# A megakernel of linear attention and a gated feed-forward: the down projection in seven products for all eight pieces, and squares added on GpSimd ahead of the norms

## What is computed

```python
def fwht(x):                      # normalised Walsh-Hadamard transform over the last axis
    ...
xn = _layernorm(x)                                   # x: (8, 512, 512) f32
q, k, v = xn @ Wq.T + bq, xn @ Wk.T + bk, xn @ Wv.T + bv
kv_sum = cumsum((elu(k) + 1) * v, axis=1)
s = ((elu(q) + 1) * kv_sum * SCALE_A) @ Wo.T + bo
y = fwht(xn * SU_ug) / 64                            # 512 wide
up = y @ W_up.T * (Wscale_up * 64)                   # 2048 wide
gate = y @ W_gate.T * (Wscale_gate * 64)
z = fwht(silu(gate) * up * SU_dp) / 64               # 2048 wide
down = z @ W_down.T * (Wscale_dp * 64)               # 512 wide
out = x + s * silu(down)
```

## Time and profile before

| | |
|---|---|
| median of 3 runs | 1291.22 us (1289.54 to 1293.17) |
| the profiled execution's own time | 1291.18 us |
| its span | 1289.4 us |
| PE, PEld | 1259.5 us (98%), 570.7 us (44%) |
| DVE, ACT, POOL | 936.1 us (73%), 618.3 us (48%), 108.9 us (8%) |
| matmuls | 5896 |
| granted TensorE clock | 1.00 of full speed |
| moved by DMA | 226.21 MB, mean 175 GB/s |

### The profile page before, as it was taken

How to read it: one execution, slowest core, us unless ns; L and a number is a source line. 1 busy time by engine, 2 the same in 40 slices (tenths; PEclk the granted TensorE clock), 3 DMA queues, 4 the chain that set the end, 5 groups by cost and what they waited for, 6 DMA issues and landing times.

```text
span 1289.4 us, 16166 instructions
## 1 busy us (share of the span) xinstructions
PE 1259.5 (98%) x5896; PEld 570.7 (44%) x5896; DVE 936.1 (73%) x1417; ACT 618.3 (48%) x912; POOL 108.9 (8%) x159
## 2 busy tenths in 40 slices
PE   5999999999999999999999999999999999999998
PEld 3544444444444444444444444444444444444443
DVE  6989989878656777777883778776773767775724
ACT  5894655532245655552334555554233655454212
POOL 1000001131210000120022001000001000000001
PEclk9999999999999999999999999999999999999999
DMA  9534775777757356575378333323526433332423
GB/s 370 224 131 125 242 215 186 241 251 292 229 205 237 113 196 231 220 251 196 131 229 257 134 128 134 131 99 103 205 93 196 145 117 116 113 129 76 130 95 103
DMA packets 65472, 226.21 MB, mean 175 GB/s; under 512 B 7408, under 2 KB 17904, under 8 KB 50800
## 3 DMA queue, kind: packets, MB, share of 16 engines
q1 hardware_dynamic: 41840, 170.64, 36.7%
q0 software_dynamic: 16272, 42.48, 11.9%
q10 hardware_dynamic: 7280, 12.06, 2.7%
HBM read 171.64 MB, written 53.50 MB: 175 GB/s over the span
## 4 chain that ended last, share of the span: by engine, by line
PE 78%; DVE 9%; issue 5%; ACT 5%; DMA 3%; SPq 0%; DVEq 0%; ACTq 0%
PE bank L2450 40%; PE bank L2636 13%; PE bank L2330 12%; PE bank L2516 7%; PE bank L2541 2%; PE bank L2661 2%; ACT work L1229 1%; ACT work L1232 1%; DMA h_all<-scr_f 1%; DVE work L1675 1%; PE bank L2375 1%; PE bank L2561 1%; DVE work L1659 1%; DVE work L1665 1%; DVE work L1702 1%
## 5 line engine op out<-in xcount | busy, mean ns | idle before, releaser
L2450 PE MATMUL bank<-xops,ring 128*128 128x512 f16 x2772 | 603.2, 379 | 7.4 <-DVE work L1702 2.6
L2450 PEld LDWEIGHTS bank<-xops,ring 128*128 128x128 f16 x2772 | 269.4, 98 | 340.2 <-issue 11.1
L2330 PE MATMUL bank<-xops,ring 128*128 128x512 f16 x1008 | 225.2, 379 | 0.5 <-DVE ring L1831 0.5
L1212 ACT ACTIVATE work<-bank 128x512 f32<-128x512 f32 x198 | 117.8, 595 | 214.7 <-PE bank L2450 200.2
L1659 DVE TENSOR_TENSOR work<-bank,work 128x512 f32<-128x512 f32 x198 | 133.4, 686 | 113.0 <-PE bank L2450 99.8
L2636 PE MATMUL bank<-h_all,ring 128*128 128x512 f16 x768 | 166.8, 379 | 0.2 <-DVE work L1659 0.2
L2330 PEld LDWEIGHTS bank<-xops,ring 128*128 128x128 f16 x1008 | 98.1, 98 | 123.6 <-issue 9.1
L2636 PEld LDWEIGHTS bank<-h_all,ring 128*128 128x128 f16 x768 | 75.0, 98 | 91.0 <-DVE work L1659 0.7
L1259 ACT ACTIVATE h_all<-work 128x512 f16<-128x512 f32 x116 | 70.6, 624 | 62.6 <-DVE work L1702 62.5
L1711 DVE TENSOR_TENSOR h_all<-work,h_all 128x512 f16<-128x512 f32 x116 | 79.3, 686 | 5.7 <-ACT h_all L1259 4.4
L1665 DVE SCALAR_TENSOR_TENSOR work<-work 128x512 f32<-128x512 f32 x64 | 44.1, 690 | 51.2 <-ACT work L1232 50.8
(11 more groups left out here) (284 smaller groups left out, 1323.4 us busy)
## 6 DMA issues: line engine op xcount, KB each, us to landing
ring<-scr_g SPq DMA_DIRECT2D x72, 1024.0 KB, 4.8
ring<-scr_d SPq DMA_DIRECT2D x15, 1024.0 KB, 5.8
scr_g<-ring SPq DMA_DIRECT2D x22, 512.0 KB, 4.4
h_all<-in_ug_t SPq DMA_DIRECT2D x8, 1024.0 KB, 12.9
ring<-in_down_t SPq DMA_DIRECT2D x6, 1024.0 KB, 6.5
scr_g<-ring POOLq DMA_DIRECT2D x12, 512.0 KB, 5.7
work<-in_x_t SPq DMA_DIRECT2D x6, 1024.0 KB, 7.0
scr_g<-h_all POOLq DMA_DIRECT2D x12, 512.0 KB, 2.9
```

The source lines that it names most:

```text
L1212: act.activation(tile(g, j), chain_bank(g)[:, :], ACT.Copy).then_inc(copied, 1)
L2330: mm = pe.matmul(plain_bank(g, j)[:, :], at[:, s, 2 * dh + kk, r, :], xops[:, kk, xs, PLAIN_B[dh][c], :], start=(n == 0), stop=(n == len(t ...
L2450: mm = pe.matmul(to[:, :], weight_of(slot, s, b, kk), at, start=(a == 0 and m in (P1, P2, P5)), stop=(a == 5), skip_group_check=True)
```

## The change

1. `SEVEN` becomes 8: the down projection of pairs 2 and 3 is made in seven products for all eight pieces, 24 matmuls each. `rest` and its banks go. The order of the products is now P1, P2, P6, P7, P4, P5, P3, each for d = 0 and then 1. The units of weights' sums become eight, and the ring's loads of those pairs hold eight pieces each, with seven loads in place of eight.
2. The token sums of pieces 6 and 7 are laid down in `xops`, in blocks that the pair's last group has just finished with: ACT's copies of piece 6 wait for P2 of group 21, those of piece 7 for P7 of it. The next pair's operands (`x_high`), which go to the same `xops`, wait for P4 of the down projection. `x_high`, `t_high` and the gates on ACT, and the adds and operands on DVE, are written in a new order.
3. P1 waits for the low part of C11 of piece 7 (before: for all of piece 5), P2 for C21 of piece 7, P6 for the sums of piece 7 (before: of piece 5), P4 for ACT's copy of P7, P3 for DVE's add of P5 to C22.
4. GpSimd adds the four blocks of squares of each piece, first two and two, then the two sums (`sum_squares`), ahead of its all-reduce for the maximum. `norm(i)` waits for that and makes 4 matmuls of one column instead of 16. Two entries of `NORM_AT` move one tile later.

```diff
-GATE_ORDER = [(d, j) for j in (C11, C22, C21, C12) for d in range(2)]
+GATE_ORDER = [(d, j) for j in (C11, C21, C22, C12) for d in range(2)]
...
-SEVEN_FROM, SEVEN = 2, 6
...
+SEVEN_FROM, SEVEN = 2, FP
+DOWN_SLOTS = (P1, P2, P6, P7, P4, P5, P3)
+DOWN_ORDER = [(d, m) for m in DOWN_SLOTS for d in range(2)]
 DOWN_COPIES = ((0, P1), (1, P1), (0, P6), (1, P6), (0, P7), (1, P7))
-DOWN_SUMS = [(d, a) for a in ("22a", "11", "22", "12") for d in range(2)]
+DOWN_SUMS = [(d, a) for a in ("11", "22", "12") for d in range(2)]
...
-NORM_AT = (6, 7, 8, 8, 9, 10, 10, 11)
+NORM_AT = (6, 7, 8, 9, 10, 10, 11, 11)
...
+IN_RES = 6
...
+        def homes_late(i, s):
+            b = (T2, T3)[i - IN_RES]
+            return xops[:, :, s, b, :], xops[:, i - IN_RES, s, B21, :]
...
             def load_x(p):
                 sp.wait_ge(h_ready, 32 * p)
+                if p > SEVEN_FROM:
+                    sp.wait_ge(hidden_sums_ready, sums_of_hidden(p - 1, SEVEN - 1))
...
             def load_last_res():
+                sp.wait_ge(seven_done, down_to(PAIRS - 1, 1, P5))
...
+            def sum_squares(i):
+                at = squares(i).rearrange("p (m k n) -> p m k n", m=2, k=KB)
+                pool.wait_ge(squared, i + 1)
+                pool.tensor_tensor(at[:, :, 0:2, :], at[:, :, 0:2, :], at[:, :, 2:4, :], ALU.add).then_inc(squares_paired, 1)
+                pool.wait_ge(squares_paired, i + 1)
+                pool.tensor_tensor(at[:, :, 0, :], at[:, :, 0, :], at[:, :, 1, :], ALU.add).then_inc(squares_summed, 1)
...
             load_blocks(0)
+            for i in range(FP):
+                sum_squares(i)
             pool.wait_ge(max_ready, 1)
...
@@ ACT, x_high
+                        act.wait_ge(seven_done, down_to(p - 1, 1, P4))
...
@@ ACT, hidden_sums_high
-                elif i >= 4 and p < PAIRS - 1:
+                elif 4 <= i < IN_RES and p < PAIRS - 1:
                     act.wait_ge(stats_taken, 2 * p + 2)
...
+                act.wait_ge(product_done, products_to(p, GROUPS - 1, (P2, P7)[i - IN_RES]))
+                two, third = homes_late(i, HI)
+                act.activation(two, work[:, at:at + 2, :], ACT.Copy)
+                act.activation(third, work[:, at + 2, :], ACT.Copy).then_inc(hidden_sums_hi, 1)
...
@@ ACT, seven_and_o
-                if p < PAIRS - 1:
-                    x_high(p + 1, 0)
-                    t_high(p + 1, 0)
-                    x_high(p + 1, 1)
-                    t_high(p + 1, 1)
                 for d, j in GATE_ORDER:
+                    if p < PAIRS - 1:
+                        if (d, j) == (0, C21):
+                            x_high(p + 1, 0)
+                        elif (d, j) == (0, C22):
+                            t_high(p + 1, 0)
+                            x_high(p + 1, 1)
+                        elif (d, j) == (0, C12):
+                            t_high(p + 1, 1)
                     seven_gate(p, d, j)
...
@@ DVE, seven_and_o
+                for d in range(2):
+                    seven_add(p, d, "11")
                 if p < PAIRS - 1:
                     x_sums(p + 1, 0)
                     t_low(p + 1, 0)
-                for d in range(2):
-                    seven_add(p, d, "22a")
-                if p < PAIRS - 1:
-                    x_sums(p + 1, 1)
-                    t_low(p + 1, 1)
-                for d, a in DOWN_SUMS[2:]:
-                    seven_add(p, d, a)
+                seven_add(p, 0, "22")
+                if p < PAIRS - 1:
+                    x_adds(p + 1, 1)
+                seven_add(p, 1, "22")
+                if p < PAIRS - 1:
+                    x_low(p + 1, 1)
+                    t_low(p + 1, 1)
+                for d in range(2):
+                    seven_add(p, d, "12")
...
@@ DVE, last_sums
                 hidden_low(p, g, C21)
+                if p >= SEVEN_FROM:
+                    for part in range(2):
+                        hidden_sums(p, FP - 1, part)
+                    hidden_sums_low(p, FP - 1)
...
@@ PE, norm
-                pe.wait_ge(squared, i + 1)
+                pe.wait_ge(squares_summed, i + 1)
...
-                        for k in range(KB):
-                            mm = pe.matmul(bank[NORM_BANK][:, at:at + 1], at_squares[:, m, k, r, :], ones[:, :],
-                                           start=(k == 0), stop=(k == KB - 1))
+                        mm = pe.matmul(bank[NORM_BANK][:, at:at + 1], at_squares[:, m, 0, r, :], ones[:, :],
+                                       start=True, stop=True)
...
@@ PE, seven
                 if m == P1:
-                    pe.wait_ge(h_ready, 32 * p + 4 * SEVEN)
+                    pe.wait_ge(h_ready, 32 * p + 4 * SEVEN - 3)
                     wait_taken(pe, p, GROUPS - 2 + d, C21)
                 elif m == P2:
+                    pe.wait_ge(h_ready, 32 * p + 4 * SEVEN - 1)
                     pe.wait_ge(summed, 3 * nth(p, GROUPS - 2 + d) + 1)
                 elif m == P5:
                     pe.wait_ge(summed, 3 * nth(p, GROUPS - 2 + d) + 3)
+                elif m == P4:
+                    pe.wait_ge(seven_copied, down_copied_to(p, d, P7))
+                elif m == P3:
+                    pe.wait_ge(seven_summed, down_summed_to(p, d, "22"))
```

More of the change, by code:

```diff
@@ L220, in slot_of @@
         return RING[n % len(RING)]
-    return LATER_RING[(LOADS * (p - SEVEN_FROM) + n) % len(LATER_RING)]
+    return LATER_RING[(loads_of(p) * (p - SEVEN_FROM) + n) % len(LATER_RING)]
 def dmas_of(p, n):
-    return 2 if p >= SEVEN_FROM and GROUPS <= n < GROUPS + 2 * KB else 1
-ALL_LOADS = [(p, n) for p in range(1, PAIRS) for n in range(LOADS)]
+    return 2 if p >= SEVEN_FROM and GROUPS <= n < GROUPS + len(DOWN_SLOTS) else 1
+ALL_LOADS = [(p, n) for p in range(1, PAIRS) for n in range(loads_of(p))]
 def loads_into(p, n):
@@ L733, in load_seven @@
                         sp.wait_ge(unit_stored[u], 16 * UNITS)
-                if m == R11:
-                    to = ring[:, slot, :].rearrange("p (c e n) -> p c e n", c=2, e=KB)
-                    for half in range(2):
-                        sp.dma_start(to[:, half, :, :], scr_d[2 * half + 1, :, :, 1024 - 256 * REST:1024]) \
-                            .then_inc(slot_loaded[slot], 16)
-                    return
                 to = ring[:, slot, 0:512 * SEVEN].rearrange("p (d n) -> p d n", d=2)
@@ L866, in _ @@
             for p in range(1, PAIRS):
-                for n in range(LOADS):
+                for n in range(loads_of(p)):
                     load(p, n)
@@ L1729, in hidden_sums_low @@
                 dve.tensor_tensor(at[:, LO, :], tile(g, C12), at[:, HI, :], ALU.subtract).then_inc(h_ready, 1)
-                three = work[:, 4 * (g % 3):4 * (g % 3) + 3, :]
+                a = 4 * (g % 3)
                 dve.wait_ge(hidden_sums_hi, sums_of_hidden(p, i))
-                dve.tensor_tensor(home(i)[:, :, LO, :], three, home(i)[:, :, HI, :], ALU.subtract) \
-                    .then_inc(hidden_sums_ready, 1)
+                if i < IN_RES:
+                    dve.tensor_tensor(home(i)[:, :, LO, :], work[:, a:a + 3, :], home(i)[:, :, HI, :], ALU.subtract) \
+                        .then_inc(hidden_sums_ready, 1)
+                    return
+                (two_high, third_high), (two, third) = homes_late(i, HI), homes_late(i, LO)
+                dve.tensor_tensor(two, work[:, a:a + 2, :], two_high, ALU.subtract)
+                dve.tensor_tensor(third, work[:, a + 2, :], third_high, ALU.subtract).then_inc(hidden_sums_ready, 1)
             def use(p, g, j):
@@ L2480, in group @@
                     for d, m in DOWN_ORDER[1:]:
-                        if m < R11:
-                            seven(p, d, m)
-                        else:
-                            rest(p, d, m)
+                        seven(p, d, m)
                 elif g + 1 == GROUPS:
```

80 lines of the change are left out of this document (32 added, 48 removed).

## The result

| | before | changed |
|---|---|---|
| median | 1291.16 us (4 runs, 1289.54 to 1293.17) | 1327.71 us (4 runs, 1326.81 to 1328.88) |
| ratio | | 1.0283, 95% interval 1.0265 to 1.0301 |
| profiled execution: time, span | 1291.18, 1289.4 us | 1327.84, 1326.0 us |
| matmuls | 5896 | 5776 |
| granted TensorE clock, mean | 1.00 | 0.985 |

The account below looks back on a forecast made before the run. PE's list of matmuls was taken to bound the kernel (busy 1259.5 of 1289.4 us). Terms 16.3 - 5.2 - 0.3 + 8.2 + 4.4 = +23.4 on 1291.2 gave 1314.6 us, range 1297 to 1332.

Parts of the forecast that it names:

- Start and switches: Norms on GpSimd: a switch of instruction kind costs 9.35 us, before the first add (start 40.35) and before the all-reduce.
- Duration of a block: Norms: GpSimd's two adds per block take 3.6 us, between 2.0 and 5.3; PE leaves the last norm 14.4 us late.
- my first rival: Norms: GpSimd adds and two-input SBUF DVE instructions exclude each other, 14 us taken, 1329 us in all; chance 0.23.
- Which path ends the stretch: First pair: last norm, all-reduce, DVE's scales (+16.7 us), then ACT's K reads make PE 16.3 us late.
- P1's wait: Sevens: P1 waits for the eighth piece's low tile behind DVE's queue, +4.1 us in each of two pairs, +8.2.
- P3's wait: Sevens, third pair alone: P3 waits for DVE's late add of C22, +4.4 us.
- The clock: Rival: after each PE wait above 4 us the clock falls, four times, 10.4 us in all, 1325 us; chance 0.12.
- Matmuls and units: Sevens: 24 fewer matmuls, -5.2 us, one wait gone, -0.3; two more units of weights' sums costed at nothing.
- Cover holds: Rival: helpers have room at each new wait, so PE pays only its matmuls, 1283 us, faster; chance 0.07.

Follow-up runs that it names:

- the runs with one add: Kernel before plus only GpSimd's first add of squares per block, norms of 8 matmuls: 1305.39 us; with four DVE adds moved later too: 1302.19 us.
- the repaired kernel: Changed kernel with norms of before, piece 6 sums later, C22 adds earlier, last group's C11 tile ahead of the add awaiting P5: 1287.21 us, ratio 0.9965.
- the two kernels with such waits: Changed kernel with only the norms as before: 1301.09 us; the same with DVE's adds of C22 moved ahead: 1297.19 us.
- the filled: Changed kernel with norms as before, plus 15 unused matmuls ahead of P1 in both pairs and P3 in the third: 1296.73 us, ratio 1.0046.

## Why the prediction came out as it did

Direction and range were right (1297 to 1332, 0.88 for slower), the time was 13 us short. By its own steps:

- **Start and switches.** I took 9.35 for each. The first measured 8.11 (39.13 in place of 40.35), the second 5.86. Both were too high, by 1.2 and 3.5 us; the first of these hid a little of the next error.
- **Duration of a block: the step that failed.** I took 3.6 for the middle of 2.0 and 5.3. Alone it would have been a good figure: 3.3. But five of the eight took 5.1, one 4.6, the first and the last 4.1, in turns with DVE. PE left the last norm 22.8 us late, not 14.4. Of GpSimd's 38.5 us from first add to last, 8 x 3.3 = 26.4 are the adds' own; 12 are exclusion. This was my first rival, at 0.23. Its 1329 us lie only 1.3 from the measured time, but by luck: it priced exclusion alone, and of the 13 us missing from the forecast 9.2 are the clock. I had weighed it down because the trace of before, as I read it, showed GpSimd's powers beside adds that read a bank or beside nothing. One of the three does lie beside a DVE instruction with two inputs in SBUF:

```profile
798.46 1.69 POOL L895 TENSOR_TENSOR rstd<-var_eps,minus_half 128x8 f32<-128x8 f32 x1 [16.68 <-DVE var_eps L1550]
```

```profile
799.48 0.68 DVE L1729 TENSOR_TENSOR h_all<-work,h_all 128x512 f16<-128x512 f32 x1
```

Neither of them is longer for it. The evidence was thus a little better than I wrote, and still not enough: a power of 8 elements says nothing of adds of 1024. Why it does not keep DVE waiting as those do, no run here shows.
- **Which path ends the stretch.** I followed PE's last norm, the all-reduce, DVE's scales and ACT. Here the last norm itself decided, 22.8 against 21.3 for the scales; my term had it the other way about. With shorter adds the scales, through DVE's own queue, decide (the runs with one add), a path that I had not priced at all: I had stretched GpSimd only.
- **P1's wait:** 4.1 twice forecast (the terms listed there add up to 3.9), 3.63 twice measured. The size was right, the reason half right. I named the seventh piece's sums; they are 0.75 of it, and the other 2.9 is DVE waiting in order for P5. The queue that I listed had "one add" in it, and I gave it a duration but not its releaser.
- **P3's wait:** 4.4 forecast (its listed terms add up to 4.6), 3.84 measured, and the cause confirmed by moving DVE's adds.
- **The clock:** costed at nothing in the sum, a rival at 0.12 with 10.4 us. Measured 1.7 behind the norms and 3.0, 2.9 and 1.6 in the sevens, 9.2 in all. Rival and forecast were both true, so their terms should have been added: a forecast with four such waits in it owed the clock something. That 9.2 is close to the rival's 10.4 is partly luck: its price was taken from transposes in a stretch whose granted clock reads 1.00, and its condition, waits above 4 us, was not met by any of the four (3.20 to 3.84). The Trainium skill's "TensorE: Matmul & The Clock Gate" (Part 1) said that idle PE falls to half its clock; by that rule, the trace agrees, with a granted clock of 0.64 behind the wait.
- **Matmuls and units:** -5.5 came in full (1285.7 and two waits of 0.48 make 1286.7, the repaired kernel took 1287.2), and no wait took the place of the units' cover at the end of the second pair.
- **Cover holds (0.07):** false as changed, true of the sevens once two queues are reordered.

On exclusion, the Trainium skill's "SBUF — State Buffer" ("Who interferes with whom") states that a DVE instruction with two SBUF inputs contends with a GpSimd instruction that reads SBUF, and one with at most one, outside the two-port modes, does not. By that rule, the trace agrees on both points: 3.08 against 1.22 us, and 0.74 unchanged. It states too that whoever issues first holds the shared ports for the whole instruction; the alternating lengths look just so, while the power above, 1.69 us long with a DVE add of 0.68 starting inside it, does not fit that if its recorded length is taken as it stands.

## What to carry to other kernels

Before giving work to an engine that looks idle, ask whom it keeps waiting: here GpSimd's adds, given to an engine that was 8% busy, delayed DVE, 73% busy, by 20 us in 40 (39.49 to 79.28, before 39.46 to 58.95). When a wait appears, look at what the releasing engine itself stands in; a helper that waits in order for the waiting engine's own last product is cured by order alone. And price a wait of some microseconds on PE as more than its length: put other matmuls in it, or expect the lower clock behind it (here up to 3.0 us behind a wait of 3.6).

## What the runs showed of the hardware that was not expected

- The stretch at the lower clock behind a wait of 3.6 to 3.9 us costs nothing, 1.6 to 1.7, or 2.8 to 3.0 us, at different places and in different kernels that have the same wait. With the norms of before, the two kernels with such waits scatter over 5 us, the filled and the repaired one over 2. What decides between the three is not shown. Behind the two waits of 2.88 us it cost 1.7 and nothing.
- GpSimd's add of 1024 bfloat16 elements a partition takes 2.12 us and that of 512 takes 1.15; an add of 8 float32 elements takes 0.20. Beside DVE's adds the last becomes 1.18.
- The switch between GpSimd's kinds of instruction took 7.4 to 8.8 us ahead of the adds and 5.8 to 6.3 ahead of the all-reduce, and it runs while the engine waits for a semaphore: in the kernel with one add for each block the last add ends at 63.27, and the all-reduce starts at 74.14, 0.13 us behind the DVE instruction that it waits for.
